# First attention: scores of a head pair by one fp32r product over 96 stacked rows of high and low parts

## The chip, the cores and the metric

The kernel runs on one core of a Trainium2 chip. The metric is the device time of one execution in microseconds (us). The kernel before takes 1415.54 us, the median of 3 runs (1415.48 to 1417.61).

## The reference

Two layers over 16 sequences of 256 tokens with 256 features, and a context of 77 rows for each sequence. Each layer is a cross attention and a mixture of experts, all with residuals. The change touches the attention of the first layer, which has 16 heads of 16 features and a layer norm over each head's queries and keys:

```python
qh = (q @ Wq.T + bq).reshape(B, QN, H, DH).transpose(0, 2, 1, 3)
kh = (k @ Wk.T + bk).reshape(B, KN, H, DH).transpose(0, 2, 1, 3)
vh = (v @ Wv.T + bv).reshape(B, KN, H, DH).transpose(0, 2, 1, 3)
qh = layernorm(qh, q_gamma, q_beta) * scale
kh = layernorm(kh, k_gamma, k_beta)
attn = jax.nn.softmax(jnp.einsum('bhqd,bhkd->bhqk', qh, kh), axis=-1)
x = jnp.einsum('bhqk,bhkd->bhqd', attn, vh)
...
x = x + _L0_xattn_ref(_layernorm(x, axis=-1), ctx_1024, ctx_1024, ...)
x = x + _L0_ffn_ref(_layernorm(x, axis=-1), ...)
```

Here B = 16, QN = 256, KN = 77, H = 16, DH = 16. Everything is float32.

## The kernel before

Each engine runs a program written out by hand, in steps; an operation of step s works on an older piece by a fixed skew. Engines wait on semaphores. `At` (line 37) is an index that may hold a loop register, `steps` (line 69) unrolls the first steps, loops over the middle and unrolls the last.

**First stage, `qkv_phase`** (line 249). It makes keys, values and queries of the first attention for all tokens. There are 8 key pieces (two sequences each) and 16 query pieces (two tiles of 128 tokens each). A class `HeadNorm` does a piece: `project` on the tensor engine PE (lines 186 to 188), `square` on the scalar engine ACT (197), `variance` on the vector engine DVE (204), `root` on ACT (211), `scale` on DVE (217 and 221), `transpose` on PE (231), and `affine` on ACT (239), one ACTIVATE that applies gamma and beta and writes keys to `kT_all` and queries to `qT_all` in SBUF, features on the partitions. Beside that DVE normalises the next tokens (373 to 385) with an inverse root by POOL (108, 110), PE transposes them (445), and ACT copies them out (413). The DMA queue of SP loads the tokens (315), running ahead as buffers come free. Of the four banks of the projection and the single bank of the transposes, the latter is free again when `affine` has read it.

**Attention, `attention0_phase`** (line 489). The unit is a half: 128 queries of one sequence with one group of 8 heads; there are 64 halves, u = 0 to 63. In half u PE does the scores (777), for u - 1 it transposes the probabilities, 8 heads (788), for u - 2 it multiplies with the values (805), and on every second half follow the transposes and products of an older tile: 814, 823, 841 on even halves, 833 and 852 on odd ones. The scores are two fp32 products of 128 queries by 4 heads x 77 keys = 308 columns over 128 rows, 8 heads x 16 features, where the keys stand in a block-diagonal form, so that a row of another head meets a zero:

```python
for a in range(2):
    last = pe.matmul(ps_s[:, a, 0:HW], q_s[p][:, gr * P:(gr + 1) * P],
                     kblk[b.mod(2)][:, (2 * gr + a) * HW:(2 * gr + a + 1) * HW],
                     start=True, stop=True)
```

POOL makes that form: `kblk` (630), two instructions per sequence that multiply the keys by the mask `hmask`, and a copy `q_s` of each tile's queries (623). DVE takes the maximum of each head's scores (665) and subtracts it (670); there is one buffer for scores in PSUM (`ps_s`), so PE's scores of u + 1 wait for the subtraction of u. ACT takes the exponent (735) and copies the transposed probabilities (730). DVE has the tile's other work after that: 679, 683, 699, 132, 137 on odd halves, 159 (the normalised rows `at_xn`, which wait for POOL's inverse root, 108 and 110), 706, 480 to 485 on even ones. POOL further copies the values (636), adds the bias to the input rows (649), and with ACT (723, 762) splits the experts' weights, already in SBUF, into a high and a low part (640), one chunk per half. SP loads input rows (578) and stores the results (602, 604).

`fp32r` is a type of four bytes in which PE takes an operand rounded. The first mixture of experts uses it: there the weights and activations are split into high and low parts and three products are summed (lines 1475, 1496, 1497 and 1500, 512 or 256 columns wide). No product in the kernel before has fp32r operands and fewer than 256 columns.

Of the kernel before, what the change touches and what calls it, by code (L numbers as in the profile page):

```python
# [16 lines left out]
P = 128  # L17
# [148 lines left out]
class HeadNorm:  # L166
# [4 lines left out]
    def __init__(self, sb, sem, g, name, rows, w, ones, bias, gamma, beta, eps, ps_p, ps_t):  # L171
        self.g, self.rows, self.w, self.bias, self.gamma, self.beta = g, rows, w, bias, gamma, beta
        self.ones = ones
        self.eps, self.ps_p, self.ps_t = eps, ps_p, ps_t
        self.sq, self.n = ([sb(f"{name}_{n}{i}", [P, 2 * D]) for i in range(2)] for n in ("sq", "n"))
        self.var, self.sd, self.rstd = (
            [sb(f"{name}_{n}{i}", [P, 2 * H]) for i in range(2)] for n in ("var", "sd", "rstd"))
        self.s_proj, self.s_sq, self.s_var, self.s_sd, self.s_rstd, self.s_n, self.s_t, self.s_out = (
            sem(f"{name}_{n}") for n in ("proj", "sq", "var", "sd", "rstd", "n", "t", "out"))
# [45 lines left out]
    def transpose(self, pe, i):  # L225
        p, r = i.mod(2), self.rows
        pe.wait_ge(self.s_n, i.n + 1)

        wait(pe, self.s_out, i.n)
        for c in range(2 * DC):  # L230
            last = pe.transpose(self.ps_t[:, c * r:(c + 1) * r], self.n[p][0:r, c * P:(c + 1) * P],
                                self.g.ident[0:r, 0:r])
        last.then_inc(self.s_t, 1)

    def affine(self, act, i, out, s_passed):

        n = 2 * DC * self.rows
        wait_alone(act, self.s_t, i.n + 1, s_passed)
        act.activation(out[:, bass.ds(i.n * n, n)], self.ps_t[:, 0:n], ACT.Identity,
                       bias=self.beta, scale=self.gamma).then_inc(self.s_out, 1)  # L240


def qkv_phase(nc, g):

    ctx = ExitStack()
    with ctx:
# [16 lines left out]
        xn = [sb(f"xn{i}", [P, 2 * D]) for i in range(2)]  # L263
# [10 lines left out]
        passed = [sem(f"passed_{n}") for n in ("dve", "pool", "act")]  # L274
        ps_p, ps_t, ps_xt, ps_v = g.bank[0:4], g.bank[4], g.bank[5:7], g.bank[7]
        k = HeadNorm(sb, sem, g, "k", LK, wk, ones3, bias3[:, 0:D], gb[:, 2:3], gb[:, 3:4], eps, ps_p, ps_t)
        q = HeadNorm(sb, sem, g, "q", P, wq, ones3, bias3[:, D:2 * D], scaled[:, 0:1], scaled[:, 1:2], eps, ps_p, ps_t)
# [22 lines left out]
        def _(sp):  # L300
            sp.dma_start(bias[:, :], g.ins["bkq"].rearrange("o (h d) -> (o h) d", d=DH)).then_inc(s_b, 16)
            sp.dma_start(wk[:, :], g.ins["wk"]).then_inc(s_wk, 16)
            for dst, src in ((wv, g.ins["wv"]), (gb, g.ins["gb"]), (bv, g.ins["bv"]), (g.ident, g.ins["ident"]),
                             (g.hmask, g.ins["hmask"])):
# [7 lines left out]
            def load_x(s):  # L312

                wait(sp, x_norm, s.shift(-3).n)
# [2118 lines left out]
```

## Time and profile before

| what | value |
|---|---|
| median of 3 runs | 1415.54 us |
| the profiled execution: its own time | 1416.21 us |
| its span in the trace | 1414.3 us |
| PE busy over the span | 1286.1 us, 91% |
| DVE, ACT, POOL busy | 918.5, 657.7, 715.3 us |
| first stage | 0 to 110.5 us |
| attention of the first layer | 110.5 to 371 us |

The profiled execution took 1.9 us more than its span, and 0.7 us more than the median. Busy times are unions over an engine's instructions. A row of a timeline gives the start in us, the duration in us, the engine, the line, the operation, the tiles out <- in, their shapes, a count where several instructions of a line are merged, and in brackets the idle time of the engine before it with what ended it. Matmuls overlap, so their pace is read from start to start: an fp32 product stands in the trace as two records.

### The profile page before, as it was taken

The numbers are of one execution on the slowest core, as the hardware profiler recorded it, in microseconds if no ns is written. First come the engines' busy times: TensorE is split into PE (matmuls) and PEld (weight loads), VectorE is DVE, ScalarE is ACT, GpSimd is POOL, SyncE is SP. The second block draws the span as 40 slices with busy tenths as digits, with TensorE's granted clock in tenths as the row PEclk, the third lists the DMA queues.
The fourth block names the chain that finished last, engine by engine and source line by source line (L and its number), as shares of the span: only waits on it lengthen the run. The fifth ranks groups of instructions, "written<-read, shape, count | busy, mean of one in ns | idle before, by whom it ended". The sixth has DMA issues, their size and how long they took to land. (4 is left out here: it accounts for less than half of the span.)

```text
span 1414.3 us, 29515 instructions
## 1 busy us (share of the span) xinstructions
PE 1286.1 (91%) x7733; PEld 1026.7 (73%) x7734; DVE 918.5 (65%) x2179; ACT 657.7 (47%) x1386; POOL 715.3 (51%) x903
## 2 busy tenths in 40 slices
PE   7997999999779999999998599857999999859998
PEld 4665777777448888888886477525888888747786
DVE  4784888888656777777776688692333333346665
ACT  2464777777325454544544477454333333221120
POOL 1223566565214655565554466306555555167775
PEclk9998999999799999999999699858999999979999
DMA  3118322222624555555554787535555556664443
GB/s 98 53 37 311 112 86 90 89 82 97 243 101 129 158 157 165 167 156 158 168 163 115 253 234 229 193 149 201 164 162 159 162 162 147 144 212 131 131 132 117
DMA packets 125980, 212.73 MB, mean 150 GB/s; under 512 B 17802, under 2 KB 92571, under 8 KB 122588
## 3 DMA queue, kind: packets, MB, share of 16 engines
q1 hardware_dynamic: 94276, 137.52, 31.5%
q0 software_dynamic: 20640, 56.39, 14.5%
q10 hardware_dynamic: 11000, 18.06, 3.4%
q8 instruction: 29, 0.48, 0.2%
q14 instruction: 35, 0.29, 0.1%
HBM read 148.03 MB, written 59.64 MB: 147 GB/s over the span
## 5 line engine op out<-in xcount | busy, mean ns | idle before, releaser
L1222 POOL DMA_INDIRECT xg<-t_xn,token x160 | 151.7, 948 | 154.6 <-PE psum L2120 70.6
L2196 POOL DMA_INDIRECT su_yg<-t_y,slot x128 | 122.8, 959 | 70.1 <-issue 38.1
L2132 PE MATMUL psum<-gu,m_xT 128*128 x640 | 153.0, 382 | 0.0
L2091 DVE TENSOR_TENSOR m_h<-psum,m_sg 128x256 f32<-128x256 f32 x80 | 33.9, 424 | 157.8 <-ACT m_sg L2070 157.8
L2132 PEld LDWEIGHTS psum<-gu,m_xT 128*128 128x128 f32 x640 | 116.6, 192 | 12.8
L1475 PE MATMUL psum<-w,m_xT_high 128*128 x284 | 119.0, 419 | 0.0
L1497 PE MATMUL psum<-m_both,m_hT_high 128*128 128x512 f32 x284 | 112.5, 418 | 1.4 <-DVE top_i L1441 1.3
L1475 PE MATMUL psum<-w_low,m_xT_high 128*128 x284 | 112.8, 397 | 0.0
L1475 PE MATMUL psum<-w,m_xT_low 128*128 x284 | 112.6, 397 | 0.0
L1348 POOL DMA_INDIRECT t_y<-top_v,dest x36 | 67.8, 1883 | 70.1 <-DVE top_v L1441 69.8
L1422 DVE TENSOR_TENSOR m_both<-w,m_both 128x1024 fp32r<-128x1024 f32 x71 | 87.0, 1225 | 14.1 <-ACT m_both L1390 10.9
L1348 POOL DMA_INDIRECT t_y<-top_i,dest x35 | 62.7, 1791 | 62.5 <-DVE top_i L1441 58.2
L730 ACT ACTIVATE at_prT<-psum 77x1024 f32<-77x1024 f32 x64 | 65.3, 1021 | 59.9 <-PE psum L788 59.9
L1397 ACT ACTIVATE m_h<-psum 128x512 f32<-128x512 f32 x71 | 42.6, 600 | 104.6 <-PE psum L1475 104.6
L1427 DVE TENSOR_TENSOR m_h<-psum,m_h 128x512 f32<-128x512 f32 x71 | 49.1, 692 | 62.3 <-ACT m_h L1397 62.3
L1213 POOL DMA_INDIRECT xg<-t_xn,token x54 | 52.7, 976 | 70.9 <-POOLq L1231 49.1
L777 PE MATMUL psum<-at_kblk,at_q_s 128*128 128x308 f32 x256 | 82.6, 446 | 5.9 <-POOL at_kblk L630 3.2
L2153 PE MATMUL psum<-dn,m_hT 128*128 x320 | 82.7, 381 | 1.6 <-DVE m_y L2099 1.4
L2063 ACT ACTIVATE m_xT<-psum 128x512 f32<-128x512 f32 x80 | 47.8, 597 | 74.0 <-PE psum L2120 74.0
L1895 ACT ACTIVATE sh_sg<-psum 128x512 f32<-128x512 f32 x32 | 19.1, 597 | 124.4 <-PE psum L1860 124.4
L2099 DVE COPY m_y<-psum 128x512 f32<-128x512 f32 x80 | 55.3, 692 | 32.6 <-PE psum L2153 16.9
L1390 ACT ACTIVATE m_both<-w 128x1024 fp32r<-128x1024 f32 x71 | 74.7, 1053 | 1.6 <-PE psum L1497 1.6
(309 smaller groups left out, 3467.3 us busy)
## 6 DMA issues: line engine op xcount, KB each, us to landing
w<-in_w SPq DMA_DIRECT2D x71, 512.0 KB, 3.8
t_y<-m_y SPq DMA_DIRECT2D x80, 256.0 KB, 2.2
w<-in_w SPq DMA_DIRECT2D x8, 1024.0 KB, 11.3
t_x<-at_x SPq DMA_DIRECT2D x64, 128.0 KB, 2.0
t_w_low<-at_low ACTq DMA_DIRECT2D x64, 128.0 KB, 1.7
w_low<-t_w_low SPq DMA_DIRECT2D x8, 1024.0 KB, 13.3
at_yg<-t_y SPq DMA_DIRECT2D x32, 256.0 KB, 3.3
gu<-in_gu ACTq DMA_DIRECT2D x8, 1024.0 KB, 12.4
```

What stands on the lines that cost most here:

```text
L730: act.activation(prT[p][0:LK, :].rearrange("p (a k) -> p a k", a=2), ps_tp[0:LK, :, :], ACT.Copy)\
L777: last = pe.matmul(ps_s[:, a, 0:HW], q_s[p][:, gr * P:(gr + 1) * P], kblk[b.mod(2)][:, (2 * gr + a) * HW:(2 * gr + a + 1) * HW], start=Tru ...
L1222: pool.indirect_dma_start(out=g.xg1[j % GB][:, k * D:(k + 1) * D], out_offset=None, in_=g.xn4, in_offset=bass.IndirectOffsetOnAxis(ap=g.to ...
L1348: pool.indirect_dma_start(out=g.y0, out_offset=bass.IndirectOffsetOnAxis(ap=g.dest[:, j:j + 1], axis=0), in_=y[p][:, :], in_offset=None).t ...
L1390: act.activation(part(p, 0), whole(p), ACT.Copy).then_inc(w2_high, 1)
L1422: dve.tensor_tensor(part(p, 1), whole(p), part(p, 0), ALU.subtract).then_inc(w2_low, 1)
L1475: last = pe.matmul(ps_gu[p][:, half, :], x[p][:, tile], w[:, at], start=(c == 0 and w is w13_high and x is xT_high), stop=(c == DC - 1 and ...
L1497: last = pe.matmul(ps_y[:, :], hT_high[p][:, tile], both[p][:, at:at + 2 * D], start=(c == 0), stop=(c == MC - 1))
L2099: dve.tensor_copy(y[p][:, :], ps_y[p][:, :]).then_inc(y_out, 1)
L2132: last = pe.matmul(ps_gu[p][:, k * 2 * M1:(k + 1) * 2 * M1], xT[p][:, at:at + P], g.gu[:, bass.ds(ex[k] * (DC * 2 * M1) + c * 2 * M1, 2 * ...
L2153: last = pe.matmul(ps_y[p][:, k * D:(k + 1) * D], hT[j.mod(HELD)][:, k * P:(k + 1) * P], g.dn[:, bass.ds(ex[k] * D, D)], start=True, stop= ...
L2196: pool.indirect_dma_start(out=yg[p][k][:, :], out_offset=None, in_=g.y1, in_offset=bass.IndirectOffsetOnAxis(ap=g.slot[:, at:at + 1], axis ...
```

## The change

The scores come from fp32r products over 96 rows. The queries of a head pair (2 heads x 16 features = 32 rows) are stacked three times: high, high, low parts; the keys of the pair, block-diagonal over 2 heads x 77 = 154 columns, as high, low, high. One product then sums high x high, high x low and low x high. A half has 4 such products (4 head pairs) in place of the two of 308 columns.

The parts are made in the first stage. `affine` becomes two ACTIVATEs from the same PSUM bank, one to fp32 and one to fp32r (the high part); a new `part` on POOL subtracts them; a new `store` on SP writes high and low parts to DRAM. `load_queries_keys` reads them back, spread over the partitions, into a ring of 4 slots of one sequence each, 9 DMAs per sequence: slots 0 to 3 in the last steps of the first stage, the others from the attention's loop on SP. POOL clears the four key slots at the start. SP's loads of tokens now stand step by step between its stores. `affine` waits until the store of the piece two before has landed, and the first stage ends when all stores have landed. `q_s`, `kblk`, `hmask` and its load are gone. Buffers move (parts and `xn` of the first stage to the space of `w2`), PE's loop of the attention is unrolled over 16 halves in place of 8, SP's over 8 tiles in place of 2, and the semaphores of the first stage and the attention have a group of their own, cleared after the attention behind a barrier.

```diff
     def transpose(self, pe, i):
...
-    def affine(self, act, i, out, s_passed):
...
+    def affine(self, act, i, s_passed):
+
+        p, n = i.mod(2), 2 * DC * self.rows
+        wait(act, self.s_low, i.shift(-1).n)
+        wait(act, self.st[p], i.div(2).n * 32)
         wait_alone(act, self.s_t, i.n + 1, s_passed)
-        act.activation(out[:, bass.ds(i.n * n, n)], self.ps_t[:, 0:n], ACT.Identity,
-                       bias=self.beta, scale=self.gamma).then_inc(self.s_out, 1)
+        for out in (self.full, self.high):
+            last = act.activation(out[p], self.ps_t[:, 0:n], ACT.Identity, bias=self.beta, scale=self.gamma)
+        last.then_inc(self.s_out, 1)
+
+    def part(self, pool, i):
+
+        p = i.mod(2)
+        pool.wait_ge(self.s_out, i.n + 1)
+        pool.tensor_tensor(self.low[p], self.full[p], self.high[p], ALU.subtract).then_inc(self.s_low, 1)
+
+    def store(self, sp, i):
+
+        p, n = i.mod(2), 2 * self.rows
+        for which, (rows, s_made) in enumerate(((self.high[p], self.s_out), (self.low[p], self.s_low))):
+            sp.wait_ge(s_made, i.n + 1)
+            sp.dma_start(self.stored[which].rearrange("(c p) t -> p c t", p=P)[:, :, bass.ds(i.n * n, n)],
+                         rows.bitcast(F32).rearrange("p (c t) -> p c t", c=DC)).then_inc(self.st[p], 16)
+
+QK_LOADS, QK_RING = 9, 4
+
+def load_queries_keys(sp, g, b, slot):
+
+    landed = g.s_qk[slot]
+    for j, part in enumerate((0, 0, 1)):
+        sp.dma_start(g.q3[slot][32 * j:32 * j + 32, :].bitcast(F32).rearrange("p (h t) -> p h t", h=HG),
+                     g.q_parts[part].rearrange("(h p) t -> p h t", p=32)[:, :, bass.ds(b.n * SQ, SQ)]).then_inc(landed, 16)
+    for j, part in enumerate((0, 1, 0)):
+        for a in range(2):
+            at = 32 * j + DH * a
+            sp.dma_start(
+                g.k3[slot][at:at + DH, :].bitcast(F32).rearrange("p (h a k) -> p h a k", h=HG, a=2)[:, :, a, :],
+                g.k_parts[part].rearrange("(h a p) k -> a p h k", a=2, p=DH)[a][:, :, bass.ds(b.n * LK, LK)])\
+                .then_inc(landed, 16)
...
         def _(sp):
...
+            def step(s):
+                i = s.shift(-4)
+                if i.within(NQP) and not (i.loop is None and i.off < 4):
+                    load_x(i)
+                if (at := piece(s, OUT + 1)) is not None:
+                    at[0].store(sp, at[1])
+                if s.loop is None and 0 <= s.off - LAST < QK_RING:
+                    b = s.off - LAST
...
+                    load_queries_keys(sp, g, At(None, 0, b), b)
+
+            steps(sp, FIRST, LAST, TOTAL + 1, BODY, step)
+            for st in q.st:
+                sp.wait_ge(st, NQP // 2 * 32)
...
             def tile(s):
                 t = s
+                b = t.div(2).shift(QK_RING - 1)
+                if t.mod(2) == 0 and b.within(NB) and not (b.loop is None and b.off < QK_RING):
+                    sp.wait_ge(s_mm, b.shift(1 - QK_RING).n * 4)
+                    load_queries_keys(sp, g, b, b.mod(QK_RING))
...
-                    pe.wait_ge(k_ready, b.n * 2 + gr + 1)
-                    pe.wait_ge(q_ready, t.n + 1)
+                    b = t.div(2)
+                    slot, a = b.mod(QK_RING), t.mod(2)
+                    pe.wait_ge(g.s_qk[slot], (b.div(QK_RING).n + 1) * 16 * QK_LOADS)

                     wait(pe, sub_done, u.n)
-                    for a in range(2):
-                        last = pe.matmul(ps_s[:, a, 0:HW], q_s[p][:, gr * P:(gr + 1) * P],
-                                         kblk[b.mod(2)][:, (2 * gr + a) * HW:(2 * gr + a + 1) * HW],
-                                         start=True, stop=True)
+                    for i in range(HG // 2):
+                        h = gr * (HG // 2) + i
+                        last = pe.matmul(ps_s[:, i // 2, i % 2 * 2 * LK:(i % 2 + 1) * 2 * LK],
+                                         g.q3[slot][0:96, h * SQ + a * P:h * SQ + (a + 1) * P],
+                                         g.k3[slot][0:96, h * 2 * LK:(h + 1) * 2 * LK], start=True, stop=True)
                     last.then_inc(s_mm, 1)
```

The order of instructions moves at two places. The first is POOL in the loop of the attention. Before, one sequence begins so (`at_q_s` is the copy of the queries, `at_kblk` the block-diagonal keys, `w<-kv` the copy of the values, `at_low` the low part of a weight chunk, `at_xb` the input rows with the bias):

```order
L623 COPY at_q_s<-qT_all 128x256
L102 ISA
L630 ISA
L630 TENSOR_TENSOR at_kblk<-kv,hmask 128x616
L630 ISA
L630 TENSOR_TENSOR at_kblk<-kv,hmask 128x616
L636 ISA
L636 COPY w<-kv 77x272
L639 ISA
L640 ISA
L640 TENSOR_TENSOR at_low<-w,at_low 128x256
```

With the change the copy of the values comes first, and nothing stands before it:

```order
L697 ISA
L697 COPY w<-kv 77x272
L700 ISA
L701 ISA
L701 TENSOR_TENSOR at_low<-w,at_low 128x256
L707 REGISTER_ALU
L86 ISA
L710 TENSOR_TENSOR at_xb<-at_x_in,at_bp 128x256
```

Three instructions per sequence and one copy per further tile have left POOL; the rest keeps its order.

The second place is SP at the end of the first stage. Before, SP had nothing after its loads of tokens, and the attention's loads followed. With the change the stores of the query pieces (`t_q_high`, `t_q_low`) have the nine loads of a ring slot between them (`q` and `k` are slots):

```order
L263 DMA t_q_high<-w 128x2x256
L263 DMA t_q_low<-w 128x2x256
L274 DMA q<-t_q_high 32x8x256 x2
L274 DMA q<-t_q_low 32x8x256
L279 DMA k_50<-t_k_high 16x8x77 x2
L279 DMA k_50<-t_k_low 16x8x77 x2
L279 DMA k_50<-t_k_high 16x8x77 x2
L263 DMA t_q_high<-w 128x2x256
L263 DMA t_q_low<-w 128x2x256
```

This pattern stands four times, and four pairs of stores follow it; the same nine loads stand before the input rows of every second tile in the attention's loop.

## Rows read from the trace of the kernel before

**Rows 1.** Busy time by stretch: start:end, length, engines with counts, PE's clock, DMA
```profile
55.00:104.00 49.00, 48.40 (x256) 34.79 (x255) 42.82 (x119) 29.02 (x57) 11.13 (x24) 1.00 0.17 50
...
180.00:355.00 175.00, 174.33 (x1693) 138.59 (x1686) 150.29 (x377) 133.11 (x260) 106.75 (x173) 1.00 0.27 89
```
**Rows 2.** Timeline of PE in the attention, one tile (two halves)
```profile
199.99 1.20 PE L777 MATMUL psum<-at_kblk,at_q_s 128*128 128x308 f32 x4
201.03 1.04 PE L788 MATMUL psum<-ident,w 128*77 128x128 f32 x8
...
207.47 1.20 PE L777 MATMUL psum<-at_kblk,at_q_s 128*128 128x308 f32 x4
```
**Rows 3.** Timeline of PE in the first experts: fp32r products of 256 columns
```profile
500.31 0.28 PE L1500 MATMUL psum<-m_both,m_hT_low 128*128 128x256 f32 x1
500.42 0.28 PE L1496 MATMUL psum<-m_both,m_hT_low 128*128 128x256 f32 x1
500.54 0.39 PE L1497 MATMUL psum<-m_both,m_hT_high 128*128 128x512 f32 x1
```
**Rows 4.** Timeline of PE's weight loads: products of 8 columns, then the scores
```profile
203.16 0.53 PEld L841 LDWEIGHTS psum<-at_wr,at_xnT 128*128 128x128 f32 x4
...
203.61 0.82 PEld L777 LDWEIGHTS psum<-at_kblk,at_q_s 128*128 128x128 f32 x4
```
**Rows 5.** Timeline of DVE in the attention, over two tiles
```profile
215.49 0.43 DVE L132 BATCH_NORM_STATS2 at_ln_stats<-at_x 128x6 f32<-128x256 f32 x1
...
217.74 0.77 DVE L159 TENSOR_SCALAR at_xn<-at_x,at_ln_mv,at_ln_rstd 128x256 f32<-128x256 f32 x1
218.77 0.17 DVE L706 COPY at_lg<-psum 128x8 f32<-128x8 f32 x1 [0.26 <-PE psum L841]
...
222.41 0.42 DVE L699 TENSOR_TENSOR at_x<-psum,at_xb 128x256 f32<-128x256 f32 x1 [0.17 <-PE psum L833]
...
225.21 1.17 DVE L159 TENSOR_SCALAR at_xn<-at_x,at_ln_mv,at_ln_rstd 128x256 f32<-128x256 f32 x1
...
229.99 0.42 DVE L699 TENSOR_TENSOR at_x<-psum,at_xb 128x256 f32<-128x256 f32 x1 [0.24 <-PE psum L833]
230.45 0.43 DVE L132 BATCH_NORM_STATS2 at_ln_stats<-at_x 128x6 f32<-128x256 f32 x1
```
**Rows 6.** Timeline of POOL in the same two tiles
```profile
217.63 0.73 POOL L640 TENSOR_TENSOR at_low<-w,at_low 128x256 fp32r<-128x256 f32 x1
...
225.01 2.44 POOL L630 TENSOR_TENSOR at_kblk<-kv,hmask 128x616 f32<-128x616 f32 x2
```
**Rows 7.** Timeline of all engines in one query step of the first stage
```profile
79.33 0.60 PE L231 MATMUL psum<-ident,qkv_q_n 128*128 128x128 f32 x4
...
80.14 0.78 ACT L239 ACTIVATE qT_all<-psum,qkv_scaled 128x512 f32 x1 [0.92 <-PE psum L231]
...
81.43 0.69 DVE L204 TENSOR_REDUCE qkv_q_var<-qkv_q_sq 128x32 f32<-128x512 f32 x1
...
82.04 0.73 DVE L373 TENSOR_SCALAR qkv_xn<-w,qkv_mv,qkv_rstd 128x256 f32<-128x256 f32 x2
...
82.74 0.60 PE L231 MATMUL psum<-ident,qkv_q_n 128*128 128x128 f32 x4
...
83.18 0.60 PE L445 MATMUL psum<-ident,qkv_xn 128*128 128x128 f32 x4
```
**Rows 8.** The same timeline, end of the first stage and start of the attention
```profile
109.50 0.78 ACT L239 ACTIVATE qT_all<-psum,qkv_scaled 128x512 f32<-128x512 f32 x1 [1.31 <-PE psum L231]
110.53 0.35 SPq L567 DMA_DIRECT2D at_wp<-in_wp  x1
...
112.21 2.42 PE L777 MATMUL psum<-at_kblk,at_q_s 128*128 128x308 f32 x4 [2.84 <-POOL at_kblk L630]
```
**Rows 9.** DMA view, 140 to 340 us: queue with packets, MB, share; issues to landing
```profile
q1 hardware_dynamic: 11476, 11.89, 18.2%
...
t_x<-at_x SPq DMA_DIRECT2D x27, 128.0 KB, 1.9
```

More of the change, by code:

```diff
@@ L174, in __init__ @@
         self.eps, self.ps_p, self.ps_t = eps, ps_p, ps_t
+        n = 2 * DC * rows
+        at = [parts[:, i * n:(i + 1) * n] for i in range(6)]
+        self.full, self.high, self.low = at[0:2], *([a.bitcast(F32R) for a in at[i:i + 2]] for i in (2, 4))
+        self.stored = stored
         self.sq, self.n = ([sb(f"{name}_{n}{i}", [P, 2 * D]) for i in range(2)] for n in ("sq", "n"))
@@ new lines, in store @@
+    def store(self, sp, i):
[11 more added lines that the diff above has]
+    for j, part in enumerate((0, 1, 0)):
+        for a in range(2):
+            at = 32 * j + DH * a
[3 more added lines that the diff above has]
+                .then_inc(landed, 16)
@@ L329, in _, with step @@
             pool.memset(g.v_all[:, :], 1.0).then_inc(s_v1, 1)
-            def invert(s):
-                p = s.mod(2)
-                wait_alone(pool, ln_mv, s.n + 1, passed[1])
-                inverse_root(pool, rstd[p][:, :], mv[p][:, :].rearrange("p (a n) -> p a n", a=2)[:, :, 1],
-                             g.minus_half[:, 0:2], ln_eps, ln_rstd, s)
-            steps(pool, 2, NQP, NQP, 2, invert)
+            for slot in range(QK_RING):
+                pool.memset(g.k3[slot][:, :].bitcast(F32), 0.0).then_inc(s_zero, 1)
+            def step(s):
+                if (i := pair(s, X)) is not None:
+                    p = i.mod(2)
+                    wait_alone(pool, ln_mv, i.n + 1, passed[1])
+                    inverse_root(pool, rstd[p][:, :], mv[p][:, :].rearrange("p (a n) -> p a n", a=2)[:, :, 1],
+                                 g.minus_half[:, 0:2], ln_eps, ln_rstd, i)
+                if (at := piece(s, OUT)) is not None:
+                    at[0].part(pool, at[1])
+            steps(pool, FIRST, LAST, TOTAL, BODY, step)
         @block.vector
@@ L503, in attention0_phase @@
         bp = sb("bp", [P, D])
-        q_s = [sb(f"q_s{i}", [P, D]) for i in range(2)]
-        kblk = [sb(f"kblk{i}", [P, NG * HG * LK]) for i in range(2)]
         spare = g.w2[:, W2_LATE * W2_COLS:]
@@ L604, in tile @@
                     sp.dma_start(g.xn[bass.ds(t.n * P, P), :], xn[p][:, :]).then_inc(xn_st[p], 16)
-            steps(sp, 6, NT, NT + 4, 2, tile)
+            steps(sp, 8, NT - 8, NT + 4, 8, tile)
             for p in range(2):
@@ L853, in half @@
                     last.then_inc(x_t, 1)
-            steps(pe, FIRST, NU, TOTAL, BODY, half)
+            steps(pe, FIRST, NU, TOTAL, 2 * BODY, half)
 CHUNKS = 64
@@ L2274, in __init__ @@
             scratch[n] for n in ("xn", "xn4", "y0", "y1", "beta", "w13_low"))
+        self.q_parts, self.k_parts = ([scratch[n + part] for part in ("_high", "_low")] for n in ("q", "k"))
 def program(nc, dram_in, out, scratch):
@@ L2286, in program @@
         g.minus_half = sb("minus_half", [P, H])
-        g.hmask = sb("hmask", [P, HG])
         g.top_v = sb("top_v", [P, NT * 8])
```

88 lines of the change are left out of this document (47 added, 41 removed).

## Prediction

> **What bounds the kernel now.** I read the busy times by stretch first, then the timelines of the two stages that the change touches. The rest of the program, from 371 us on, keeps its code, so only those stages are costed.
>
> In the attention PE sets the pace: it is busy 174.33 of 175 us, DVE 150.29, ACT 133.11, POOL 106.75 [rows 1]. The timeline of PE gives the period: the scores of two successive even halves start at 199.99 and 207.47, so a tile takes 7.48 us and a half 3.74. In a half the scores take 201.03 - 199.99 = 1.04 us, start to start [rows 2]. So whatever is saved on the scores is a gain until the next engine stops it, and the next one is DVE. Its timeline over two tiles, 215.49 to 230.45, is 14.96 us, and in it DVE waits for PE only 0.26 + 0.17 + 0.24 = 0.67 us [rows 5]. The reader should see that 150 of 175 us understates DVE: its other gaps are waits for its own previous result, which a faster PE does not shorten.
>
> In the query steps of the first stage PE (48.40 of 49 us) and DVE (42.82) are both close to full, ACT (29.02) and POOL (11.13) are not [rows 1]. A step is 82.74 - 79.33 = 3.41 us [rows 7].
>
> **The scores.** The nearest rows for a product of 154 fp32r columns are from two sides. fp32r products of 256 columns start 0.11 and 0.12 us apart [rows 3]. fp32 products of only 8 columns follow one another by (203.61 - 203.16) / 4 = 0.11 us [rows 4], so with a full load of 128 columns ahead of each, few columns cost no less than 256 do. From above, fp32 itself: 1.04 us for 616 columns is 0.26 us for 154. I take 0.117, from the rows of the same type, which the 8 columns meet from below: 4 x 0.117 = 0.47 us in place of 1.04. PE's half falls by 0.57 to 3.17 us.
>
> DVE then bounds. Without its waits for PE two tiles take 14.96 - 0.67 = 14.29 us. One thing gets shorter: the normalised rows (159) took 0.77 us where POOL had just begun a low part of 0.73, and 1.17 where it had begun the block-diagonal keys, 2.44 for two [rows 5, 6]. Those keys are gone, the low part stays, so 0.40 per two tiles goes: 13.89 us, or 3.47 per half. Of the 64 halves I count 57 in this state: 57 x (3.74 - 3.47) = **-15.5 us**. Bounds: without that relief 14.29 / 4 = 3.57, -10 us; with DVE wholly covered, PE's 3.17, -33.
>
> **The front of the attention.** PE starts its first scores at 112.21, 1.7 us after the stage began with SP's 110.53, because POOL must make the keys [rows 8]. Now they are already loaded. In the other seven halves of the front PE is not full: the scores, the maximum, the subtraction and the next scores are a ring, since there is one buffer of scores, and the ring loses the 0.57 us of the product: 4 us. Together **-6**, between -1.7 and -8.
>
> **Loads and stores in the attention.** A sequence (four halves) adds 9 DMAs, 9 x 0.35 = 3.2 us of issue on SP [rows 8], and 3 x 256 + 6 x 128 = 1536 packets. The queue's packets took 18.2% of 16 engines over 200 us, 582 us for 11476, 0.051 each [rows 9]; so 1536 of them take 4.9 us on 16 engines, in a period of some 14 us, beside a share of 0.27 that is used [rows 1]. The loads run three sequences ahead, and in SP's program only input rows and stores stand behind them, with more than a half of slack. Zero; were it not covered, PE would wait at the scores for the slot.
>
> **The first stage, each step.** ACT gets a second ACTIVATE of 0.78 us (0.75 where two follow each other). It waited 0.92 us before the first one, so ACT has the time, but behind it stand the square, DVE's variance (81.43) and the next normalisation (82.04) [rows 7]; the latter moves back 0.75 us. POOL's new subtraction, twice the 256 columns of 0.73 us [rows 6], runs from about 2.3 to 3.8 us after PE's transposes, and the normalisation would now begin at 3.46, so it also meets that. What the rows show of such a meeting is the 0.77 or 1.17 us of line 159, where the same shape takes 0.73 / 2 = 0.37 alone [rows 5 to 7]: it ends with POOL's instruction. That is 0.35 more. The slack to PE's transposes of the tokens at 83.18 is 0.4 [rows 7]. So 0.75 + 0.35 - 0.4 = 0.7 us remain, on a path that spans two steps: 0.35 a step, 14 steps, **+5** (0 to +9).
>
> The Trainium skill, "SBUF — State Buffer", section "Who interferes with whom", says that DVE in a two-port mode and POOL exclude each other for a whole instruction, and whoever issues first holds the port pair; the trace agrees, with the 1.17 us above. By that rule alone a subtraction that always started just before the normalisation would cost 1.46 us a step in place of my 0.35, and the sum would be some 12 to 15 us higher. I keep 0.35 since the ends of the two are fixed to the same transposes; the other is the third rival.
>
> **The end of the first stage.** The last three pieces are a chain (PE transposes, ACT, PE again, with one PSUM bank), so three times 0.75 = 2.3 us. After the last ACTIVATE the stage ended at once (109.50 + 0.78, SP at 110.53 [rows 8]); now follow POOL's subtraction 1.46, a DMA issue 0.35 and its landing 1.9 [rows 6, 8, 9]: 3.7. ACT also waits for the store of the piece two before, and SP has 4 x 3.2 us of loads to issue between those stores: 2 us. **+8**, between +6 and +15. One load less at the start (`hmask`), POOL's clears (done before its first subtraction) and one more barrier I cost at nothing; the barriers of today show 0.25 us.
>
> **Sum.** -15.5 - 6 + 5 + 8 = -8.5 against the profiled execution's 1416.21 us gives 1407.7; that execution is 0.7 over the median, so **1407 us** on the scale of the runs. The case's own range, with the bounds not all at one end, is 1394 to 1417.
>
> **Rivals.** *First: a narrow fp32r product runs at fp32's pace.* No row has fp32r under 256 columns; 0.26 us each would make 1.04 per half as before. For it: four weight loads and 616 columns stay, only the type changes. Against it: the fp32 rows pay their price as two records per product, and nothing at 256 columns hints at a step. PE's half stays 3.74, POOL's relief is worth nothing under a full PE, of the front only the 1.7 remains: -1.7 + 13 = +11, **1426 us**. It decides the sign where a product costs over about 0.23 us (then the 57 halves return less than the 7 us that are needed beyond the front). Chance 0.33.
>
> *Second: DVE does not bind.* The 0.17 and 0.26 us gaps may hide more, and line 159 fall to 0.37 when POOL is early; then PE's 3.17 sets the half: -33 - 6 + 13 = -26, **1390 us**. Against it: 13.89 us counted from a timeline with few gaps. Chance 0.11.
>
> *Third: POOL's subtraction holds up DVE in the first stage,* 1.2 us a step or more, or the stores wait behind the loads for as long: the stage costs 25 instead of 13 and the sum is about +3.5, **1419 us**. Against it: the fixed phase argued above. Chance 0.12.
>
> **How the numbers follow.** The forecast's case has 0.44. Faster by over 0.2% (2.8 us, about what a measurement of this kernel can tell from no change): 0.39 of the first case, 0.11 of the second rival, together 0.50. Within 0.2%: 0.04 of the forecast, 0.04 of the first rival at its low bounds and 0.04 of the third, 0.12. Slower: 0.38, mostly the first rival. The range 1389 to 1429 us takes in the second rival's value, the third, and the first up to +13.
>
> **What would show it.** Right: in the attention the four products of a half start 0.11 to 0.13 us apart, a half takes about 3.47 us, DVE waits for PE at no row and PE waits for DVE's subtraction; the copies of queries and keys are gone from POOL; the attention starts about 13 us later than 110.5, with steps of about 3.75 in the first stage. Products 0.26 us apart would show the first rival; a half of 3.2 us the second; normalisations of over 1 us in the first stage, or stores that land 5 us and more after their issue, the third. A wait of PE for `s_qk` in the attention would make the zero of the loads wrong.

## The result, and the profile after

The changed kernel takes 1450.6 us (median of 4 runs, 1450.09 to 1451.56) against 1415.5 of the kernel before beside it: ratio 1.025, 95% interval 1.0231 to 1.027. The forecast was 1407 us, so the sign is wrong too. Profiled span: 1447.2 us against 1414.3, +32.9.

Where these 32.9 us lie, by the starts of ACT's `square` of the queries and of PE's score products in the timelines of both kernels:

| stretch | before, us | after, us | difference | predicted |
|---|---|---|---|---|
| up to the first query step's square | 53.56 | 55.19 | +1.6 | 0 |
| first to 16th square (15 steps) | 50.64 | 63.43 | +12.8 | +5 |
| 16th square to the first score product | 8.01 | 19.61 | +11.6 | +8, and -1.7 of the front |
| scores: 1st to 9th half | 28.40 | 30.03 | +1.6 | -4.3, the rest of the front |
| 9th to 21st half | 44.42 | 50.56 | +6.1 | |
| 21st to 49th half | 104.70 | 104.91 | +0.2 | -15.5 for the three |
| 49th to 64th half | 55.99 | 58.39 | +2.4 | |
| last score product to the end | 1068.6 | 1065.1 | -3.5 | 0 |

(The last row's code is the same in both; the experiments that compute the same have 1065 to 1073 there, so it is scatter of single executions.)

Busy time by stretch in the changed kernel; the first and third row answer to [rows 1], the second is the end of the first stage:

```profile
55.00:104.00 49.00, 42.64 (x216) 28.84 (x214) 37.70 (x107) 31.81 (x61) 24.69 (x36) 1.00 0.56 171
104.00:138.00 34.00, 12.72 (x58) 8.59 (x57) 8.71 (x18) 13.63 (x24) 9.79 (x9) 0.70 0.99 227
180.00:355.00 175.00, 157.18 (x1595) 127.14 (x1588) 148.32 (x357) 125.32 (x243) 67.37 (x121) 0.95 0.59 153
```

PE, full before, is not full in either stage now; the DMA engines went from 0.17 to 0.56 and from 0.27 to 0.59, and to 0.99 between the stages.

**A step of the first stage,** timeline (answers to [rows 7]):

```profile
79.42 1.27 POOL L256 TENSOR_TENSOR w<-w 128x512 fp32r<-128x512 f32 x1 [2.17 <-ACT w L249]
...
80.66 0.22 POOL L108 TENSOR_SCALAR qkv_rstd<-qkv_mv 128x2 f32<-128x2 f32 x1
...
80.96 0.71 POOL L110 TENSOR_TENSOR qkv_rstd<-qkv_rstd,minus_half 128x2 f32<-128x2 f32 x1
...
81.80 0.74 DVE L443 TENSOR_SCALAR w<-w,qkv_mv,qkv_rstd 128x256 f32<-128x256 f32 x2 [1.17 <-POOL qkv_rstd L110]
...
82.67 0.65 PE L515 MATMUL psum<-ident,w 128*128 128x128 f32 x4 [0.96 <-DVE w L443]
```

POOL's subtraction (256) stands ahead of the inverse root (108, 110) on the same engine; the normalisation (443) waits 1.17 us for the root, and PE 0.96 for the normalisation. The steps take 3.8 and 4.6 us in turn instead of 3.41.

**The end of the first stage,** timeline (answers to [rows 8]):

```profile
113.25 1.05 SPq L274 DMA_DIRECT2D q<-t_q_high  x2
...
117.28 1.45 ACT L249 ACTIVATE w<-psum,qkv_scaled 128x512 f32<-128x512 f32 x2 [2.54 <-DMA t_q_low<-w]
...
117.79 0.43 SPq L263 DMA_DIRECT2D t_q_high<-w  x1
...
123.62 1.45 ACT L249 ACTIVATE w<-psum,qkv_scaled 128x512 f32<-128x512 f32 x2 [3.33 <-DMA t_q_low<-w]
...
129.86 1.45 ACT L249 ACTIVATE w<-psum,qkv_scaled 128x512 f32<-128x512 f32 x2 [4.80 <-DMA t_q_low<-w]
132.74 1.45 ACT L249 ACTIVATE w<-psum,qkv_scaled 128x512 f32<-128x512 f32 x2 [1.43 <-POOL w L256]
...
138.23 1.10 PE L839 MATMUL psum<-k,q 96*128 96x154 f32 x4 [5.70 <-PEq L288]
```

SP issues a slot's nine loads from 113.25 to 117.7 between two pairs of stores, and each of the three ACTIVATEs from 117.28 to 129.86 waits until an earlier store has left its buffer. The DMA view of 104 to 130 us shows a full queue and landings of 4.6 us (1.9 in [rows 9]):

```profile
q1 hardware_dynamic: 9250, 6.54, 116.3%
...
t_q_low<-w SPq DMA_DIRECT2D x5, 256.0 KB, 4.6
```

**The attention,** timelines of ACT, PE, POOL and DVE over one sequence's boundary (answers to [rows 2, 5, 6]):

```profile
240.72 0.72 ACT L796 ACTIVATE w<-w 128x616 f32<-128x616 f32 x1 [0.31 <-DVE w L731]
240.87 0.65 PE L839 MATMUL psum<-k,q 96*128 96x154 f32 x4
241.50 0.87 PEld L850 LDWEIGHTS psum<-ident,w 128*77 128x77 f32 x8
241.50 1.10 PE L850 MATMUL psum<-ident,w 128*77 128x128 f32 x8
...
243.46 0.41 POOL L697 COPY w<-kv 77x272 f32 x1
243.83 0.74 POOL L701 TENSOR_TENSOR at_low<-w,at_low 128x256 fp32r<-128x256 f32 x1
243.92 2.17 DVE L159 TENSOR_SCALAR at_xn<-at_x,at_ln_mv,at_ln_rstd 128x256 f32<-128x256 f32 x1
244.16 0.65 PE L839 MATMUL psum<-k,q 96*128 96x154 f32 x4
244.53 0.73 POOL L710 TENSOR_TENSOR at_xb<-at_x_in,at_bp 128x256 f32<-128x256 f32 x1
245.21 0.72 POOL L701 TENSOR_TENSOR at_low<-w,at_low 128x256 fp32r<-128x256 f32 x1
...
248.89 0.67 PE L839 MATMUL psum<-k,q 96*128 96x154 f32 x4 [1.15 <-DVE w L731]
...
252.06 0.43 DVE L159 TENSOR_SCALAR at_xn<-at_x,at_ln_mv,at_ln_rstd 128x256 f32<-128x256 f32 x1
```

From the first product to the transposes (850) it is 241.50 - 240.87 = 0.63 us, but that is not the price of the four products. Taken one by one they start at 240.87, 241.03, 241.14 and 241.25, that is 0.15, 0.11 and 0.11 us apart (0.117 predicted). Then PE waits: the transposes read the probabilities, ACT's exponential (796) ends at 240.72 + 0.72 = 241.44, and the weights of the first transpose load 0.05 us later. In all 32 halves from 203 to 322 us they load 0.05 to 0.13 us behind the end of the exponential, and the exponential starts 0.03 us behind DVE's subtraction (731); in the kernel before the transposes came 0.34 to 0.80 us behind it (38 halves from 200 to 345 us), since PE was late. So DVE sets the pace here, by the subtraction and the exponential, and PE's busy time hides the wait, since the modelled end of the last product covers it.

Three halves of a sequence take 3.2 to 3.9 us; the fourth takes 248.89 - 244.16 = 4.73, because DVE's LayerNorm (159) is held for 2.17 us until POOL's run of copy, low, addition and low is over. Four halves together take 14.7 or 15.3 us, before 14.96: what PE was given, DVE took back.

**A stall** at 183 us, DVE behind a store; DMA view of 165 to 190 us:

```profile
187.25 0.42 DVE L760 TENSOR_TENSOR at_x<-psum,at_xb 128x256 f32<-128x256 f32 x1 [4.17 <-DMA t_x<-at_x]
```
```profile
q1 hardware_dynamic: 5502, 6.67, 107.6%
...
t_x<-at_x SPq DMA_DIRECT2D x2, 128.0 KB, 9.9
```

A store of `t_x` lands 9.9 us after its issue. Two halves take 7.5 and 5.9 us, the second of them at a granted clock of 0.50, the lower of PE's two levels, after PE had been busy 1.26 of the 5 us from 185 to 190.

### The profile page after: what moved, and what is told of

Its sections match the earlier page's. It is cut to its first block and busy times, and to the rows that moved or that the text cites. A ratio compares the mean times of both kernels' runs of the same rounds, so it can differ in the third digit from the quotient of the medians.

```text
span 1447.2 us, 29552 instructions
## 1 busy us (share of the span) xinstructions
PE 1277.9 (88%) x7733; PEld 1024.8 (71%) x7734; DVE 925.9 (64%) x2179; ACT 673.6 (47%) x1410; POOL 697.3 (48%) x867
## 3 DMA queue, kind: packets, MB, share of 16 engines
q0 software_dynamic: 20640, 56.39, 14.1%
## 5 line engine op out<-in xcount | busy, mean ns | idle before, releaser
L2258 POOL DMA_INDIRECT su_yg<-t_y,slot x128 | 123.9, 968 | 67.4 <-issue 38.1
L2194 PEld LDWEIGHTS psum<-gu,m_xT 128*128 128x128 f32 x640 | 116.5, 192 | 12.8
L1484 DVE TENSOR_TENSOR m_both<-w,m_both 128x1024 fp32r<-128x1024 f32 x71 | 87.0, 1225 | 13.9 <-ACT m_both L1452 10.8
L850 PE MATMUL psum<-ident,w 128*77 128x128 f32 x512 | 76.8, 298 | 2.6 <-ACT w L796 1.3
L108 POOL TENSOR_SCALAR at_ln_rstd<-at_ln_mv 128x1 f32<-128x1 f32 x32 | 7.0, 220 | 143.1 <-DVE at_ln_mv L137 143.1
```

The costliest lines, as they stand in the source:

```text
L850: last = pe.transpose(ps_tp[0:LK, h // 4, (h % 4) * P:(h % 4 + 1) * P], pr[p][:, h * LK:(h + 1) * LK], g.ident[:, :])
L1484: dve.tensor_tensor(part(p, 1), whole(p), part(p, 0), ALU.subtract).then_inc(w2_low, 1)
L2194: last = pe.matmul(ps_gu[p][:, k * 2 * M1:(k + 1) * 2 * M1], xT[p][:, at:at + P], g.gu[:, bass.ds(ex[k] * (DC * 2 * M1) + c * 2 * M1, 2 * ...
L2258: pool.indirect_dma_start(out=yg[p][k][:, :], out_offset=None, in_=g.y1, in_offset=bass.IndirectOffsetOnAxis(ap=g.slot[:, at:at + 1], axis ...
```

## Experiments

Start: first score product; scores: first to last product, both from one profiled execution; time and ratio to the kernel before: all runs. Where the first stage is as in the changed kernel (3, 4, 6, 9, 12, 13), the start is 136.5 to 138.8 us. Where the loads are (1, 2, 4 to 8, 12, 13), the 9th to the 21st half, with the stall, take 49.8 to 59.2 us. Smaller differences between two runs in these columns are scatter.

| run | start, us | scores, us | time, us | ratio (95%) |
|---|---|---|---|---|
| before | 112.2 | 233.5 | 1415.5 | |
| changed kernel | 138.2 | 243.9 | 1450.6 | 1.0231 to 1.027 |
| loads early (1) | 131.5 | 245.6 | 1450.0 | 1.0213 to 1.026 |
| part late (2) | 136.6 | 245.0 | 1450.9 | 1.0213 to 1.0248 |
| no loads (3) | 138.3 | 235.3 | 1448.4 | 1.0191 to 1.0228 |
| copy on ACT (4) | 136.5 | 224.1 | 1434.6 | 1.0105 to 1.0155 |
| long runs (5) | 135.3 | 246.6 | 1450.0 | 1.0213 to 1.0252 |
| wide products (6) | 137.3 | 241.1 | 1447.8 | 1.0197 to 1.023 |
| four edits (7) | 130.6 | 223.6 | 1426.4 | 1.0055 to 1.0095 |
| tail (8) | 129.8 | 246.4 | 1445.4 | 1.0188 to 1.0224 |
| one ahead (9) | 138.0 | 234.2 | 1446.2 | 1.0206 to 1.0249 |
| combined (10) | 126.0 | 219.5 | 1413.7 | 0.9974 to 0.9997 |
| combined, two slots (11) | 123.9 | 217.7 | 1410.8 | 0.9944 to 0.9975 |
| copy last (12) | 138.8 | 226.6 | 1438.2 | 1.0129 to 1.018 |
| delay (13) | 138.0 | 231.0 | 1435.3 | 1.0104 to 1.0174 |

**1. Slot loads in the middle of the first stage.**
```diff
+EARLY, APART = 16, 2
...
-                if s.loop is None and 0 <= s.off - LAST < QK_RING:
-                    b = s.off - LAST
+                if 0 <= s.off - EARLY < QK_RING * APART and (s.off - EARLY) % APART == 0:
+                    b = (s.off - EARLY) // APART
...
-            steps(sp, FIRST, LAST, TOTAL + 1, BODY, step)
+            few(TOTAL + 1, step)
```


> SyncE's steps of the first stage are written out, and the loads of the first four slots stand in the middle of the stage (one slot every second step) instead of between its last stores. Theory, the queue: in the changed kernel the last affines wait 2.5 to 4.8 us each for stores that stand behind the loads of a slot; without that the first score product starts at about 122 us instead of 138.2, and the time is about 1435. Rival, the chain: two ACTIVATEs, the subtraction and a store one after another set the end of the stage by themselves; then the products still start after 134 us and the time stays over 1446.

Less than half of it: the start came 6.7 us earlier, not 16, and the time did not move (1450.0), as the rival had said of the time but not of the start. The waits for stores moved to where the loads now are (2.44 us at 104.34), and a second limit came out, the last steps' timeline:

```profile
120.25 1.43 ACT L249 ACTIVATE w<-psum,qkv_scaled 128x512 f32<-128x512 f32 x2
...
121.82 1.08 PE L238 MATMUL psum<-ident,qkv_q_n 128*128 128x128 f32 x4 [2.27 <-ACT w L249]
...
123.11 1.44 ACT L249 ACTIVATE w<-psum,qkv_scaled 128x512 f32<-128x512 f32 x2 [1.43 <-POOL w L256]
```

With one PSUM bank the transposes wait for the ACTIVATEs and these for the transposes, at the half clock that PE had fallen to: 2.88 us a step.

**2. The low part one step later on POOL.** The call of `part` takes `OUT + 1` instead of `OUT`.

> GpSimd makes the low part of a step one step later, behind the next step's inverse root. Theory: the inverse root that VectorE's normalisation waits for stands behind the subtraction on GpSimd, and this makes the steps of the queries 3.85 and 4.55 us long in turn; with the order turned they are about 3.5 us, and TensorE is busy over 19 of the 20 us from 60 to 80 (17.7 in the changed kernel). The end of the stage is set by the loads, so the time gains 0 to 6 us (1445 to 1451). Rival: the second ACTIVATE, or VectorE slowed by GpSimd, sets the step; then it stays near 4.2 us and TensorE at 17 to 18 of 20.

The waits for the root are gone, but a step takes 3.9 to 4.06 us, not 3.5. DVE's normalisation, by line from 60 to 80 us (mean 409 ns in the changed kernel):

```profile
L443 DVE TENSOR_SCALAR w<-w,qkv_mv,qkv_rstd 128x256 f32<-128x256 f32 x11 | 7.1, 677 | 0.0
```

It now runs beside the subtraction and is held by it: both costs of the subtraction exist, and the order only chooses which is paid. The start, 136.6, is within the scatter and the time is 1450.9: the end of the stage still waits for stores.

**3. No loads in the attention.** `load_queries_keys` of sequences 4 to 15 left out, PE waits for the first filling of a slot.

> The loads of sequences 4 to 15 in the attention are left out, and the four slots that are there are used again, so the scores of these sequences are computed from the queries and keys of others. Theory: the loads fill the queues, and the stalls behind them (VectorE's 4.2 us for a store of t_x at 183 us, a stall at 323 to 338 us) go; from the first to the last score product 236 us instead of 243.9, the time about 1443; the steady groups of four halves stay at 14.7 to 15.3 us, since no transfer sets them. Rival one: the expert weights alone fill the queues; then nothing changes by over 2 us. Rival two: the loads set the steady halves too; then these go to 13.3 us a group and the stretch to about 222.

The theory's 236 was met with 235.3: the stall at 183 us is the loads', the steady groups are not. The whole time can't be read against the others, because other scores send tokens to other experts later.

**4. The values' copy on ACT.** `pool.tensor_copy(v_b...)` becomes an `act.activation(..., ACT.Copy)` ahead of the exponential.

> The copy of a sequence's values is moved from GpSimd to ScalarE. Theory: in the changed kernel the LayerNorm of every second tile takes 2.17 us on VectorE (0.43 to 0.64 in the other) because GpSimd's copy, low, xb and low run without a gap while it wants the port; without the copy it takes under 0.9, a group of four halves 13.4 us instead of 14.7 to 15.3, the first to the last product about 225 us instead of 243.9 (12 steady groups by 1.5), the time about 1432. Rival: GpSimd's other three instructions hold it as long; then L159 stays at about 2 us and the time within 3 us of 1450.6.

Confirmed: scores 19.8 us shorter, 16 us of time; steady groups of four halves mostly take 13.2 to 13.9 us. DVE's LayerNorm from 203 to 330 us (mean 1320 ns in the changed kernel), and from the 21st to the 49th a half is 3.43 us on average:

```profile
L159 DVE TENSOR_SCALAR at_xn<-at_x,at_ln_mv,at_ln_rstd 128x256 f32<-128x256 f32 x19 | 9.4, 493 | 0.0
```

PE is busy 122.81 of the 127 us from 203 to 330, yet in 29 of the 35 halves from 210 to 330 us the transposes still load 0.05 us behind the exponential. In the few where the exponential was done early, the four products show their own price, 251.68 - 251.19 = 0.49 us, 0.12 each:

```profile
250.80 0.72 ACT L793 ACTIVATE w<-w 128x616 f32<-128x616 f32 x1
251.19 0.65 PE L836 MATMUL psum<-k,q 96*128 96x154 f32 x4
251.68 1.04 PE L847 MATMUL psum<-ident,w 128*77 128x128 f32 x8
```

**5. Longer runs in DRAM.** `q_high`, `q_low` as (16 x 128, 512) instead of (256, 4096).

> The queries' parts lie in DRAM by sequence, row and head group, so that a store is 128 runs of 2 KB (before 256 of 1 KB) and a load of a part 128 runs of 2 KB (before 256 of 1 KB); bytes, DMAs and the keys are as they were. Theory: what fills the queues is the number of packets; per sequence 1152 instead of 1536 in the loads, 256 instead of 512 in the stores, so the waits of the last affines (2.5 to 4.8 us each) and the stall at 183 us shrink by about a third: the first product at about 133 us instead of 138.2, the time about 1442. Rival: bytes set it (1.75 MB of loads in the tail); then nothing moves by over 2 us.

The time did not move (1450.0). The start came 2.9 us earlier, between the theory's 5 and the rival's 2, and the scores took 2.7 us longer. In the DMA part of the page, changed kernel first, the same bytes in 10240 packets fewer take nearly the same share of the engines:

```profile
q1 hardware_dynamic: 134068, 164.81, 39.1%
```
```profile
q1 hardware_dynamic: 123828, 164.81, 38.6%
```

**6. Wide products.** `n = 2 * LK if h == HG - 1 else 256` columns of the keys.

> Seven of the eight score products of a tile read 256 columns of the keys instead of 154 (the columns too many are overwritten by the next product). It asks what a product is paid by: the changed kernel's four take 0.64 us, 0.157 each, where I had taken 0.117 from products of 256 columns. Theory, the weight load: each product waits for its own 128 columns of weights, so width costs nothing, the four stay at 0.6 to 0.7 us and the time within 3 us of 1450.6. Rival one, a price by column: 0.157 times 256/154, four products 1.0 us, a half 0.35 us more on TensorE. Rival two, narrow fp32r runs at a slower pace than 256 columns: then the four fall to 0.47 us.

From the first product to the transposes it is still 252.22 - 251.59 = 0.63 us. But both theory and rivals took this for the price of the products, and it isn't:

```profile
251.45 0.72 ACT L796 ACTIVATE w<-w 128x616 f32<-128x616 f32 x1 [0.31 <-DVE w L731]
251.59 0.67 PE L840 MATMUL psum<-k,q 96*128 96x256 f32 x4
252.22 1.10 PE L851 MATMUL psum<-ident,w 128*77 128x128 f32 x8
```

The exponential ends at 251.45 + 0.72 = 252.17, and the transposes wait for it as in the changed kernel. One by one the wide products start 0.20, 0.12 and 0.12 us apart, the narrow ones 0.15, 0.11 and 0.11. So the run shows that the width costs no time in this place, because the wait covers it; it doesn't show what a product is paid by.

**7. Edits 1, 2, 4 and 5 together.**

> Four edits together: the slot loads in the middle of the first stage, the low part a step later on GpSimd, the queries' parts in runs of 2 KB, and the values' copy on ScalarE. By the single runs: start of the products 131.5 us with the first alone; the steps of the queries near 3.5 us instead of 3.85 and 4.55 take another 5 to 8 us off, to about 124; the attention 224 us as with the copy moved, or 215 without the stall of 10 us at 183; the rest as it was (1068 us). Sum: 1407 to 1418 us, that is about as fast as the kernel before. If the four do not add up since the tail's chain stands behind them all, 1425.

They did not add up: 1426.4, near the fallback's 1425, with a start of 130.6, 0.9 us earlier than by the early loads alone. The DMA engines were full (share 1.0 to 1.1) from 90 to 110 and from 140 to 180 us, and behind the latter two halves took 11.2 and 5.9 us.

**8. The end of the first stage.** Edit 1 with `13` and `3` for its `16` and `2`, edit 2, two banks for the transposes, the last `q.st` wait moved into the attention.

> The first stage alone: slot loads one every third step from the 14th step on, the low part a step later, the transposes of the queries in turn in two PSUM banks, and the wait for the last stores moved into the attention, ahead of its first load of a slot. In the run with the loads early the last steps took 2.88 us each (two ACTIVATEs 1.45, transposes at half clock 1.09, and the gaps) and the stage ended 2.5 us behind the last store's issue. Theory: with two banks a step of the tail is ACT's 1.5 us, with no wait at the end the products start at 118 to 123 us (138.2 in the changed kernel, 131.5 with early loads alone), time 1436. Rival: 4 MB of slot loads and as much of stores must pass the 16 queues in the stage whatever the order; then the start stays over 128.

The rival's side: a start of 129.8 and 1445.4, not 1436. With all four slots inside the stage the queue is full (share 0.9 to 1.0 from 70 to 120 us) wherever they stand.

**9. One sequence ahead.** `b = t.div(2).shift(1)`, and the 12 loads for the next stage at tiles 6 and 7.

> The attention alone: a slot is loaded one sequence ahead instead of three, and the 12 loads for the next stage are issued at the 7th and 8th tile instead of ahead of the expert weights. Theory: the stall at 183 us (VectorE waits 4 to 8 us for a store of t_x, 10 us from issue to landing) is the store standing behind expert weights and slot loads of 1 MB each in the queue; with fewer of them ahead it goes, the 16th product of the stretch comes about 6 us earlier, first to last product 236 us instead of 243.9, time 1443. Rival: the stall moves to where the loads are now (tiles 7 to 10) and is as long; then 243 to 246.

The stall is gone; the scores take 234.2 us, the time is 1446.2, not 1443. Two things were moved at once, the slot loads and the 12 others, and this run doesn't tell which of them did it. A store of `t_x` lands after 4.2 us (160 to 185 us; 9.9 in the changed kernel):

```profile
t_x<-at_x SPq DMA_DIRECT2D x2, 128.0 KB, 4.2
```

**10. Edits 4, 5, 8 and 9 together.**

> The edits of the two runs beside this one together with the values' copy on ScalarE and the queries in runs of 2 KB. Start of the products 120 us, 63 halves of 3.37 us each without stalls 212 us plus 3 for the front at half clock, the rest 1068 us: 1403, that is 13 us faster than the kernel before. If the queues stay jammed in one of the two places, 1412 to 1418.

1413.7, the fallback and not the 1403: a start of 126 instead of 120, and two halves of 6.8 and 5.4 us at 182, where the next stage's loads now lie.

**11. The same with two slots in the first stage** (0 and 1), slots 2 and 3 in the attention, the next stage's loads at its last tiles.

> As the second combination, but only slots 0 and 1 are loaded in the first stage (2 MB less between its stores), slots 2 and 3 at the second and fourth tile of the attention, and the 12 loads for the next stage at its last tiles. Theory: the affines' waits for stores at the end of the stage (2.1, 2.8 and 2.2 us) and the stall at 182 us (two halves of 6.8 and 5.4 instead of 3.3) are the queue's; without them the products start at about 120 us (126.0) and the stretch of 64 products takes about 214 us (219.5): time 1403. Rival: the weights of the attention (8 MB by 165 us) jam the loads of slots 2 and 3 and TensorE waits for them; then the start gains and the stretch loses as much, 1410 to 1414.

Faster than the kernel before by 0.4% (ratio 0.996), but not 1403: the start is 123.9 instead of 120, the scores 217.7 instead of 214. The stall is gone; a wait of 1.5 us for a store is left at the end of the stage. The rows of [rows 1] again:

```profile
55.00:104.00 49.00, 44.19 (x221) 29.77 (x220) 43.57 (x110) 32.80 (x62) 25.61 (x38) 1.00 0.76 219
180.00:355.00 175.00, 166.96 (x1804) 137.24 (x1802) 149.50 (x411) 145.28 (x295) 75.47 (x130) 1.00 0.65 177
```

Some of these edits (the next stage's loads) would suit the kernel before as well; that was not tried.

**12. The copy on POOL behind the addition,** a few lines lower in the same half.

> The changed kernel with the values' copy still on GpSimd, but behind the addition of the same half instead of ahead of low and the addition. Theory: the LayerNorm of VectorE is held when it comes up right behind GpSimd's copy; with low ahead of it it starts beside low as in the tiles without a copy and takes 0.43 to 0.65 us in both; groups of four halves 13.3 to 13.7 us, time about 1434 as with the copy on ScalarE. Rival: it is the length of GpSimd's run without a gap (2.6 us with four instructions), wherever the copy stands in it; then L159 stays over 1.5 us in every second tile and the time at 1450.

Confirmed: from 210 us on L159 takes 0.41 to 0.64 us in all tiles; groups are 13.5 and 14.1 us, the time is 1438.2, 4 us over the forecast. But this edit, like 4, also moved the moment at which L159 meets `low`.

**13. An addition in place of the copy,** which goes to ACT as in run 4.
```diff
-                        pool.tensor_copy(v_b[bp_][0:LK, :], g.v_all[0:LK, bass.ds(b.n * VW, VW)]).then_inc(v_ready, 1)
...
+                    pool.tensor_tensor(idle[:, :], g.ones[:, :], g.ones[:, :], ALU.add).then_inc(s_idle, 1)
```


> The values' copy is on ScalarE, and in its place GpSimd makes an addition of 128 columns (0.35 to 0.4 us, as long as the copy) that nobody reads. It asks what holds VectorE's LayerNorm for 2.17 us. Theory, the copy: it is that kind of instruction on GpSimd; an addition in its place leaves L159 at 0.41 to 0.65 us in both tiles, groups of four halves at 13.2 to 13.8 us, time about 1435. Rival, the moment: GpSimd's low then starts 0.4 us later, so that L159 comes 0.1 us behind low's start instead of 0.45 us, and that alone holds it until GpSimd's run of additions ends; then L159 is 2.1 to 2.2 us in every second tile, groups 14.7 to 15.3, time about 1450.

Between the two, and nearer to the theory: 1435.3, groups of 13.5 and 14.1 us.

```profile
244.37 0.40 POOL L695 TENSOR_TENSOR at_idle<-ones 128x128 f32<-128x128 f32 x1
244.72 0.73 POOL L699 TENSOR_TENSOR at_low<-w,at_low 128x256 fp32r<-128x256 f32 x1
244.81 0.79 DVE L159 TENSOR_SCALAR at_xn<-at_x,at_ln_mv,at_ln_rstd 128x256 f32<-128x256 f32 x1
```

At the same moment, 0.09 us behind the start of `low`, L159 takes 0.79 us: it ends with that one instruction. With the copy ahead it takes 2.17 and ends with the whole run. So the moment costs 0.35 us and this copy 1.4 more.

It is this copy, not any copy. The kernel before has one in the same place in every second tile, that of the queries, with the same run behind it and L159 0.11 us behind the start of `low` (217.74, [rows 5]), which takes 0.77 us:

```profile
217.27 0.40 POOL L623 COPY at_q_s<-qT_all 128x256 f32 x1
217.63 0.73 POOL L640 TENSOR_TENSOR at_low<-w,at_low 128x256 fp32r<-128x256 f32 x1
218.32 0.77 POOL L649 TENSOR_TENSOR at_xb<-at_x_in,at_bp 128x256 f32<-128x256 f32 x1
219.06 0.72 POOL L640 TENSOR_TENSOR at_low<-w,at_low 128x256 fp32r<-128x256 f32 x1
```

Six such meetings from 187 to 340 us take 0.77 to 0.79. That the values' copy (77 rows by 272 columns) in this place makes the wait is shown; what in it does so, its shape or its operands, is open.

## Why the prediction was wrong

- **"Those keys are gone, the low part stays, so 0.40 per two tiles goes: 3.47 per half": this step failed, and with it -15.5.** I read L159's 0.77 and 1.17 us as "it ends with POOL's instruction" and took POOL's largest instruction away, but not what follows in its place: the copy of the values, with `low`, addition and `low` behind it without a gap. L159 went to 2.17 in one tile and 0.43 to 0.64 in the next; with 2.17 and 0.43 that is 1.06 us more per two tiles than the 2 x 0.77 in my sum, 13.89 + 1.06 = 14.95, and measured are 14.7 and 15.3. Runs 4, 12 and 13 show it. My reading of the 0.77 was right for the kernel before; what the values' copy ahead of the same `low` does to it, no row of before shows.
- **"DVE then bounds" was right.** In the steady part of the changed kernel DVE waits for PE at no row, and in every half PE's transposes wait for the exponential behind DVE's subtraction. It stays so without the copy: my 14.29 with 0.43 for both L159 is 14.29 - 0.77 - 1.17 + 0.86 = 13.21 us, and the shortest groups of runs 4 and 11 are 13.1 to 13.2 (the others up to 13.9 for the most part). The second rival (PE's 3.17 sets the half) did not come.
- **Products: 0.117 was right too,** with 0.15, 0.11 and 0.11 us from start to start and 0.12 on average (run 4's 0.49 us for four), and the first rival (0.26) wrong. What I left out is that the transposes wait for the exponential: so 0.57 to 0.83 us pass from the first product to them in the steady part, and "PE's half falls by 0.57 to 3.17 us" never showed. Under a DVE that bounds this cost the forecast nothing. In the expectation of run 6 I took that wait for the price of the products, which was wrong.
- **Loads in the attention: "Zero" failed.** I weighed 4.9 us of queue time against 14 us of period, an average. The first 50 us of the attention hold 8 MB of expert weights and the next stage's inputs too, SP has one queue for all of it, and what waited was not PE for `s_qk` but DVE for the store of `t_x` behind the loads: 6.1 us there, and 5.4 to 14.8 in the other runs that keep these loads. Run 3 removes it by leaving the loads out, run 9 by moving them and the next stage's.
- **First stage, each step: +5 against +12.8.** I placed the subtraction beside the normalisation and charged 0.35 a step. I did not look at what stands behind it on POOL: the inverse root. Where the order is turned (run 2), the meeting costs 0.27 per instruction and twice that per step. This is the third rival's mechanism, by POOL's order more than by the port, at 0.8 us a step where the rival had 1.2. The last of the 15 steps also holds a wait of 2.5 us for a store.
- **End of the first stage: +8 against +11.6.** The "2 us" for stores behind loads was the mis-sized term: two waits of 3.3 and 4.8 us (the third, 2.5, is in the steps). What follows the last ACTIVATE was about right: it ends at 134.2, and the first product starts 4.0 us later, 2.1 more than before, against 3.7 less the 1.7 of the front. Run 11, with half the loads there and the edits of run 8, has 10.1 us from the last square to the first product, 2.1 more than before.
- **The front: the -4.3 of the ring against +1.6.** PE idled through the end of the stage (busy 0.00 of the 5 us from 120 to 125), and the granted clock was 0.50, the lower of its two levels, from 120 to 165 us (in the kernel before it was 1.00 from 125 on); at it a product group takes 1.11 us instead of 0.65. I left the clock out. In run 6, with the same front, the clock was back at 150 us, and the stretch took 25.8 us, 2.6 less than before.
- **Sum and range.** Against the forecast, from one profiled execution to the other, the way to the first product cost 15 us more, the rest of the front 6, the other halves 24, and 3.5 came back at the end: 41 us. The third rival's price of the stage, 25 us, was nearly met (26.0), but I paired it with the gain in the halves, and no case had the halves lose.

The Trainium skill, "SBUF — State Buffer", section "Who interferes with whom", says that where VectorE in a two-port mode and GpSimd meet, the first to issue holds the shared ports for its instruction. Run 13's 0.79 us agrees; the 2.17 us over three instructions behind the values' copy, and the 0.43 us inside a running `low` of 0.73, are not what it says, and the measurement decides.

## What to carry to other kernels

When an instruction is taken off an engine that another one collides with, write down the new order of that engine and what now stands where the collision was; the engine's busy time falling (POOL from 106.75 to 67.37 us) says nothing about it. Moving operands through DRAM to save PE time costs the queue in the stretch where it is fullest, not on average: count all transfers of that stretch, and ask which small store stands behind them. And read what ends an interval before you call it a price: the 0.63 us from the products to the next group held a wait for another engine, which PE's busy time did not show. Whether the ring is better loaded one sequence ahead than three, as in run 9, was not tried by itself.

## What the runs showed that I had not expected

- Ahead of a gapless run of three POOL instructions, the values' copy (77x272) makes a DVE `tensor_scalar` that comes 0.09 us into the run wait for the whole of it (2.17 us); an addition of equal length (0.79) and the copy of the queries (128x256, 0.77) make it wait for one instruction only. One that comes 0.44 us into an instruction was not held (0.43 at 252.06).
- Four fp32r products of 96 rows by 154 columns take 0.49 us when nothing behind them waits, 0.12 each, near the 0.11 to 0.12 of 128 rows by 256 columns.
- In the middle of the attention, where PE is no longer full, its clock fell to the lower level for some 10 us. The windows before and after 326 us in the changed kernel; nothing waits for a transfer there, PE had waited 1.15 us for DVE at 323.73, as it does once a sequence:

```profile
316.00:326.00 10.00, 8.69 (x97) 7.04 (x99) 8.74 (x21) 7.46 (x17) 3.50 (x8) 0.99 0.51 135
327.00:337.00 10.00, 10.00 (x71) 8.55 (x69) 6.42 (x17) 5.20 (x11) 2.77 (x7) 0.55 0.31 91
```

Two halves then take 4.8 and 5.9 us where 3.8 and 3.45 are usual, and the group of four 18.3 instead of 15.3: 3 us that neither engine's work explains. Such a pair comes at other places, or not at all, in the other runs; in the kernel before, whose PE was full, there is none. What sets it off is open.
